# A recurrence kernel on one core: thirteen start loads folded to five, input and kernel pieces dealt out anew over the steps, and the products of zeros left out of the step loop

## What is computed

```python
# 1. a recurrence over time, h has 256 values for each sequence
xw = x @ Wx + b
for t in range(512): h = tanh(xw[:, t] + h @ Wh)
# 2. a long convolution; its kernel K is a sum of 64 decaying exponentials
K[m, t] = sum_n C_re[m, n] * exp(dt[m] * A[n] * t)
x = x + (h * K) + h * D
# 3. a gated scan (sigmoid gates, cumulative sums of logarithms)
# 4. 16 experts with top-2 routing, and one shared expert
```

## Time and profile before

| what | us |
|---|---|
| three timed runs | 998.55, 1029.65, 1040.39 (median 1029.65) |
| the profiled execution, device time | 1004.57 |
| its span from first to last instruction | 1002.7 |
| mean granted TensorE clock in it | 0.962 of full speed |

### The profile page before, as it was taken

One profiled execution on the slowest core, in us unless ns is written; L12 is line 12 of the kernel. 1 busy time (PEld: TensorE's weight loads), 2 busy tenths in 40 slices (PEclk: granted clock), 3 DMA queues, 4 the chain that ended last, 5 costly groups with the idle time before them and its releaser, 6 DMA issues.

```text
span 1002.7 us, 61045 instructions
## 1 busy us (share of the span) xinstructions
PE 938.8 (94%) x26800; PEld 768.1 (77%) x26800; DVE 437.5 (44%) x932; ACT 556.7 (56%) x1956; POOL 314.4 (31%) x308
## 2 busy tenths in 40 slices
PE   7999999999999997788999999999899999999994
PEld 5787777777777776577444444787899999999993
DVE  1000100010001006578398899975556464646450
ACT  3344454545544558687486767333466565656551
POOL 2111211121112112332000644573034546364555
PEclk6589999999999999899899999999999999999997
DMA  3122222234554402872100111163075757566534
GB/s 92 64 96 94 85 97 102 96 76 58 59 64 56 55 13 38 189 146 53 45 1 1 66 45 46 41 232 105 37 204 134 156 126 162 129 157 133 125 42 53
DMA packets 85347, 89.61 MB, mean 89 GB/s; under 512 B 8657, under 2 KB 71654, under 8 KB 85298
## 3 DMA queue, kind: packets, MB, share of 16 engines
q1 hardware_dynamic: 69410, 71.50, 28.3%
q0 software_dynamic: 14592, 17.10, 10.2%
q10 hardware_dynamic: 1296, 0.37, 0.2%
HBM read 56.82 MB, written 33.96 MB: 91 GB/s over the span
## 4 chain that ended last, share of the span: by engine, by line
PE 77%; issue 5%; ACT 5%; DVE 4%; POOL 4%; DMA 2%; ACTq 0%; POOLq 0%; DVEq 0%
PE ps L526 21%; PE ps L820 17%; PE ps L518 9%; PE ps L834 8%; PE ps L686 8%; PE ps L494 3%; PE ps L736 3%; POOL slots_in L457 3%; PE ps L501 2%; PE ps L745 2%; PE ps L593 2%; ACT tok L889 2%; PE ps L608 1%; DMA slots_in<-tok,arena 1%; PE ps L763 1%
## 5 line engine op out<-in xcount | busy, mean ns | idle before, releaser
L526 PE MATMUL ps<-tok,wh 128*32 128x8 f32 x16384 | 259.2, 182 | 13.5 <-issue 3.0
L526 PEld LDWEIGHTS ps<-tok,wh 128*32 128x32 f32 x16384 | 216.1, 115 | 61.2 <-ACT tok L889 25.6
L889 ACT ACTIVATE tok<-ps 128x8 f32<-128x8 f32 x1024 | 155.3, 177 | 190.1 <-PE ps L526 190.0
L476 POOL DMA_INDIRECT out<-arena,dest x80 | 127.9, 1599 | 99.3 <-ACT arena L1047 80.1
L1161 DVE TENSOR_SCALAR arena<-ps 128x127 f32<-128x127 f32 x32 | 9.3, 290 | 335.9 <-PE ps L501 335.9
L820 PE MATMUL ps<-xgT_hi,ew_hi 128*128 128x320 f32 (+1 forms) x384 | 119.5, 311 | 2.9 <-DVE spare L1302 1.6
L820 PE MATMUL ps<-xgT_hi,ew_lo 128*128 128x320 f32 (+1 forms) x384 | 119.8, 312 | 0.0
L820 PE MATMUL ps<-xgT_lo,ew_hi 128*128 128x320 f32 (+1 forms) x384 | 119.0, 310 | 0.0
L518 PE MATMUL ps<-xst,wx 128*32 128x64 f32 (+1 forms) x3120 | 106.7, 212 | 0.0
L1408 DVE TENSOR_TENSOR mid<-mid,ps 128x320 f32<-128x320 f32 (+1 forms) x96 | 46.7, 486 | 106.5 <-ACT mid L1065 104.4
L686 PE MATMUL ps<-mid,gw 128*128 128x512 f32 x192 | 86.1, 607 | 2.4 <-ACT mid L975 1.6
(11 more groups left out here) (206 smaller groups left out, 1760.7 us busy)
## 6 DMA issues: line engine op xcount, KB each, us to landing
ring<-k_pad SPq DMA_DIRECT2D x64, 256.0 KB, 6.3
slots_in<-mid SPq DMA_DIRECT2D x16, 645.0 KB, 3.6
mid<-slots_in SPq DMA_DIRECT2D x16, 645.0 KB, 4.2
arena<-in_ex_down SPq DMA_DIRECT2D x16, 384.0 KB, 3.2
arena<-in_ex_gate SPq DMA_DIRECT2D x16, 352.0 KB, 4.5
arena<-in_ex_up SPq DMA_DIRECT2D x16, 352.0 KB, 6.0
xst<-in_x_steps SPq DMA_DIRECT2D x66, 64.0 KB, 1.8
xtok<-in_x_tok SPq DMA_DIRECT2D x16, 256.0 KB, 2.7
```

The costliest lines, as they stand in the source:

```text
L476: pool.indirect_dma_start(out=out[:, :], out_offset=bass.IndirectOffsetOnAxis(ap=dest[:, z, t:t + 1], axis=0), in_=yo[:, z, t], in_offset= ...
L526: last = nc.tensor.matmul(sums_at(bank, t, o)[Q * j:Q * j + Q], wh[:, k, columns(j, o)], hring[:, (n - 1) % (2 * G), k], start=False, stop ...
L889: nc.scalar.activation(hring[:, n, o], sums_at(n // G, n % G, o), ACT.Tanh).then_inc(s_h[o], 1)
```

## The change

- Ten tables that came in ten loads (the first state `h0r` and the nine constants) lie side by side in one array `pack`, in DRAM and on chip, and come in one load of 128 rows by 737 floats, which ScalarE issues first. `wh` is loaded behind it, from ScalarE's queue and no longer from SyncE's, and `s_state` counts this load alone.
- VectorE copies the first state as soon as `pack` is there and clears `ctmp` after it.
- `keep_up(256)` is gone from the steps.
- The pieces of the inputs stand after other steps: 0 after t = 1, 1 and 2 after t = 2, 3 after t = 3, 4 and 5 after t = 4, 6 after t = 5, 7 and 8 after t = 6.
- The kernel sums stand after the steps 7 and 8, two pieces (four matmuls) each.

```diff
-        state = ((wh, wh_d), (h0r, h0_rec))
-        loads = ((a_q, a_q_d), (dt_q, dt_q_d), (a_bc, a_bc_d),
-                 (dt_bc, dt_bc_d), (c_q, c_q_d), (d_k, d_k_d), (consts, consts_d), (iota_t, iota_t_d), (rows_to, rows_to_d))
...
-        INPUTS = {1: (0, 2), 2: (2, 4), 3: (4, 5), 4: (5, 6), 5: (6, 7), 6: (7, NIN)}
+        INPUTS = {1: (0, 1), 2: (1, 3), 3: (3, 4), 4: (4, 6), 5: (6, 7), 6: (7, NIN)}
...
-            for dst, src in state:
-                sp.dma_start(dst[:], src).then_inc(s_state, 16)
...
-                    if t in (0, G - 1):
-                        keep_up(256)
-                    if 11 <= n < 11 + 2 * NH:
-                        if n == 11:
+                    if n in (G - 1, G):
+                        if n == G - 1:
                             pe.wait_ge(s_ps0, 1)
                             pe.wait_ge(s_kqe, i + 1)
                             pe.wait_ge(s_kc, i + 1)
-                        kernel_sums(n - 11)
-            pe.wait_ge(s_state, STATE_LOADED)
+                        for piece in range(NH * (n - G + 1), NH * (n - G + 2)):
+                            kernel_sums(piece)
+            pe.wait_ge(s_state, 16)
...
-            for dst, src in loads:
-                act.dma_start(dst[:], src).then_inc(s_const, 16)
+            act.dma_start(pack[:], pack_d).then_inc(s_const, 16)
+            act.dma_start(wh[:], wh_d).then_inc(s_state, 16)
...
-            nc.vector.memset(ctmp, 0.0).then_inc(s_x1, 2)
-
-            dve.wait_ge(s_state, STATE_LOADED)
+
+            dve.wait_ge(s_const, LOADED)
             for k in range(C):
                 nc.vector.tensor_copy(hring[:, 2 * G - 1, k], h0r[:, k]).then_inc(s_h[k], 1)
-            dve.wait_ge(s_const, LOADED)
+            nc.vector.memset(ctmp, 0.0).then_inc(s_x1, 2)
```

More of the change, by code:

```diff
@@ L51, with build @@
 AHEAD = EARLY - 1
-def build(nc, x_tok, x_steps, h0_rec, h0_gate, wx_d, wh_d, b_rec_d, a_bc_d, a_q_d, dt_bc_d, dt_q_d, c_q_d, d_k_d,
+def build(nc, x_tok, x_steps, h0_gate, wx_d, wh_d, b_rec_d, pack_d,
           gate_w, gate_b, router_w, router_b, sh_gate, sh_up, sh_down, ex_gate, ex_up, ex_down,
-          ident_d, consts_d, iota_t_d, tri_d, resets_d, iota_e_d, rows_to_d, out):
+          ident_d, tri_d, resets_d, iota_e_d, out):
     k_pad = nc.dram_tensor("k_pad", [D, 2 * P], F32).ap()
@@ L69, in build @@
         brow = sb("brow", [1, D])
-        h0r = sb("h0r", [P, C, B])
         h0g = sb("h0g", [P, C, B])
[L72 to L77, removed]
+        sizes = (C * B, NST, NH, NG * J, NG + KG, NG * NH, IT, 8, P, R + CT)
+        pack = sb("pack", [P, sum(sizes)])
+        h0r, a_bc, a_q, dt_bc, dt_q, c_q, d_k, consts, iota_t, rows_to = [pack[:, sum(sizes[:n]):sum(sizes[:n + 1])] for n in range(len(sizes))]
+        h0r = h0r.rearrange("p (c b) -> p c b", c=C)
+        dt_bc = dt_bc.rearrange("p (g j) -> p g j", j=J)
+        c_q = c_q.rearrange("p (g h) -> p g h", h=NH)
         dta_q = sb("dta_q", [P, NG + KG, NH])
@@ L83, in build @@
         ident = sb("ident", [P, P])
-        consts = sb("consts", [P, 8])
-        iota_t = sb("iota_t", [P, P])
         tri = sb("tri", [P, 2, P])
@@ L91, in build @@
         spare = sb("spare", [P, 512])
-        rows_to = sb("rows_to", [P, R + CT])
         share = sb("share", [P, 2, CT])
@@ L254, in build @@
         first = ((wx, wx_d), (brow, b_rec_d))
-        state = ((wh, wh_d), (h0r, h0_rec))
-        loads = ((a_q, a_q_d), (dt_q, dt_q_d), (a_bc, a_bc_d),
-                 (dt_bc, dt_bc_d), (c_q, c_q_d), (d_k, d_k_d), (consts, consts_d), (iota_t, iota_t_d), (rows_to, rows_to_d))
         late = ((ident, ident_d), (tri, tri_d), (h0g, h0_gate), (gw, gate_w), (gb, gate_b), (rw, router_w), (rb, router_b),
                 (resets, resets_d), (iota_e, iota_e_d))
-        FIRST_LOADED, STATE_LOADED, LOADED, LATE = 16 * len(first), 16 * len(state), 16 * len(loads), 16 * len(late)
+        FIRST_LOADED, LOADED, LATE = 16 * len(first), 16, 16 * len(late)
         NT = 2 * C
@@ L1484 @@
     tri = np.stack([np.triu(np.ones((P, P)), 1) - 1, np.ones((P, P))], 1).astype(f32)
+    pack = (rec(cond.T), np.broadcast_to(a_log, (P, NST)), np.tile(a_log.reshape(NH, Q).T, (J, 1)), np.broadcast_to(dt.reshape(J, NG).T, (P, NG, J)),
+            np.concatenate([np.repeat(dt.reshape(J, NG), Q, 0), np.zeros((P, KG), f32)], 1), c_re.reshape(J, NG, NH, Q).transpose(0, 3, 1, 2), d_k,
+            consts, np.broadcast_to(-np.arange(P, dtype=f32), (P, P)),
+            np.concatenate([np.arange(N, dtype=f32).reshape(P, R), N + np.arange(CAP, dtype=f32).reshape(P, CT)], 1))
     arrays = {
@@ L1487 @@
         "x_steps": np.concatenate([steps, np.zeros((2, P, C, G, B), f32)]),
-        "h0_rec": rec(cond.T),
         "h0_gate": rows(cond.T),
@@ L1492 @@
         "b_rec": np.asarray(L0_cond_b)[None],
-        "a_bc": np.broadcast_to(a_log, (P, NST)),
-        "a_q": np.tile(a_log.reshape(NH, Q).T, (J, 1)),
-        "dt_bc": np.broadcast_to(dt.reshape(J, NG).T, (P, NG, J)),
-        "dt_q": np.concatenate([np.repeat(dt.reshape(J, NG), Q, 0), np.zeros((P, KG), f32)], 1),
-        "c_q": c_re.reshape(J, NG, NH, Q).transpose(0, 3, 1, 2).reshape(P, NG, NH),
-        "d_k": d_k.reshape(P, IT),
+        "pack": np.concatenate([np.reshape(v, (P, -1)) for v in pack], 1),
         "gate_w": np.stack([rows(np.asarray(w).T) for w in (L0_cond2_W_f, L0_cond2_W_i, L0_cond2_W_h)], 1),
@@ L1509 @@
         "ident": np.eye(P, dtype=f32),
-        "consts": consts,
-        "iota_t": np.broadcast_to(-np.arange(P, dtype=f32), (P, P)),
         "tri": tri,
@@ L1514 @@
         "iota_e": np.broadcast_to(iota_e, (P, NE)),
-        "rows_to": np.concatenate([np.arange(N, dtype=f32).reshape(P, R), N + np.arange(CAP, dtype=f32).reshape(P, CT)], 1),
     }
```

## The result

The changed kernel takes 1043.59 us (median of four executions, 1040.21 to 1046.58) against 1021.56 for the kernel before (median of four, 998.55 to 1040.39). The ratio is 1.037 with a 95% interval from 1.023 to 1.051: it is slower. Unlike before, the four executions lie close together. The title's count of loads is off: before the loop 15 loads were issued, now 6, since ten became one.

A forecast was written before the change was run, and what follows sets the result against it. A two-engine ring of product and tanh, floor 0.67 us a step, bounds the loop. 1004.57 - 2.0 (start) - 9.0 (full-clock turns) - 2.4 (half-clock turns) = 991.2, plus 4 x 2.95 gives 1003 us; range 979 to 1077.

The forecast's parts named there:

- whether the clock comes back: TensorE's clock in the step loop: the rise to full clock was expected about as late as before; called the open term.
- the forecast of 1003: Whole kernel with six half-clock turns behind the first, the mean of before: 991.2 + 4 x 2.95 = 1003 us; chance 0.57.
- go for nothing at full clock: Products of zeros in the step loop: they stand where the distance is 0.67 us already, so removing them gains nothing.
- Rival A: Step loop: full clock does not come back, 29 more turns at half clock, 1077 us, slower by 4.6%; chance 0.18.
- account of its spread: Kernel before: its three timed runs fit about 0.3, 9 and 12 half-clock turns behind the first, 3.58 us a turn.
- Turns at half clock: Step loop: a turn becomes 13.8 us, 0.94 less (0.36 to 1.6); three such turns gain 2.4 us.
- Turns at full clock: Step loop: moved pieces and sums save 0.31 us a turn, to 10.85; 29 turns gain 9.0 us (0 to 12.8).
- The start: Before the loop: packed load brings the first tanh from 8.79 to 6.8 us, gain 2.0 us (0.7 to 2.1).
- chain of constants: ScalarE's start: pack lands at 5.0 us, the constants end at 6.5, so the products at 6.77 decide the first tanh.
- The first turn: Loop's first turn, partly stalled: counted among three half-clock turns gaining 2.4 us together; its stalls on issue stay.

The follow-up runs named there:

- the added branch: Twelve 512-column products of zeros behind a branch at the first turn's end: with zeros after steps 15 and 0 1024.58 us, kernel before 1030.93, changed kernel 1063.47.

## Why the prediction was wrong

**The step that failed** is the one on whether the clock comes back. I asked only when it rises, took it for granted that it then stays, and priced every case by one number of half-clock turns at the loop's start. I wrote down that the prediction fails altogether if the clock, once full, falls again inside the loop, and it fell six times: 20.3 half-clock turns behind the first, where the forecast of 1003 had six. What I had against the change ("the two steps around a turn's end have no fill any more") was the right place; I weighed it for the rise, where it is not what decides, and not for the hold. Runs with zeros back there and nowhere else kept the clock in all three profiles without the added branch. Where a rise would come I had right, behind the steps 7 to 10 of some turn.

**The clue in the rows.** The sum says that products of zeros "go for nothing at full clock", read from a distance of 0.67 that did not move. That is right for a turn and wrong for the kernel: the run without them shows the same 11.16 us turn and 66 us more in all. A matmul that nobody waits for had a use that no wait shows.

**Rival A** (no full clock in the loop) named the mechanism's family and was 33 us too high; the truth is between it and the forecast, with 20 half-clock turns behind the first instead of 31. No execution took more than the 1050 us that I had set for slower, but the 1029.65 behind that bound was too high for the kernel before; the ratio's interval, 1.023 to 1.051, says slower. The measured time lies inside the range of 979 to 1077, but the sign was wrong: I gave faster 0.45 and slower 0.22.

**The kernel before** itself had a median of 1021.56 with the fourth execution, and of 1005 to 1020 beside the later runs, not 1029.65. My account of its spread by when the rise comes fits the two profiles taken of this loop without the branch: rises at 56.0 and 115.4 us, four turns apart, which is 14 us at 3.58 a turn, and times 16 us apart.

**Turns at half clock**: 13.38 us, 0.94 was predicted as the gain and 1.36 measured, inside my 0.36 to 1.6. The zeros made 0.35 of it (14.39 us without them in the old places, 0.36 predicted), the new places the other 1.01, for which I had 0.6. **Turns at full clock**: 10.91, predicted 10.85. The floor holds behind steps 1, 2, 7 to 10, 13 and 14, better than the 0.70 that I took for 2 and 10; the back edge at 0.83 took 0.16 of it back, and I had no term for it.

**The start**: 2.0 us predicted, 0.44 measured in this pair of profiles, outside its 0.7 to 2.1. It varies: with the new start unaltered nine profiles have the first tanh at 7.51 to 8.58 us, mean 8.14, and three with the old one at 8.79 to 9.19, mean 8.98, so the gain is nearer 0.8. The pack landed early enough (ScalarE's first exponential at 4.17, I had 5.0), but I asked only whether `wh` would be late. What was late was the first input piece, which waits for `wx` among others: it came 0.87 us later and ran at half clock. The mechanism of the chain of constants was right; what was next to be late was not.

**The first turn** grew by 1.5 us where I had a small gain; its stalls on issue are longer or more (the one at 14.97 us took 0.79 before, the one at 15.79 now 1.43). It goes with the new start and not with the loop: in the run with the old loop and the new start the first turn takes 20.18 us, against 18.84 before and 20.30 in the changed kernel, and its second turn begins at 28.54 us where before it began at 27.63. So the earlier first tanh was more than lost again within the first turn. What makes the stalls longer no run tells.

The Trainium skill, "TensorE: Matmul & The Clock Gate", has in its section "A second HAM failure mode: psum-queue depth-cycling" a kernel whose short idles between groups of matmuls make the clock go to and fro, at a cost in throughput. The trace agrees: six falls between 81 and 368 us, with TensorE shown busy 16.15 of the 17.00 us before the first of them. The rule of its section "What's actually happening", that activity releases the clock, agrees with the twelve dense products, behind which it rose three times of three.

**What stays open.** Why the back edge costs 0.83 us in the changed loop and 0.67 in the loop of before; it is 0.67 in the run with ten zeros, so it is not the places of the pieces. Whether two products of zeros in other steps than 15 and 0 would hold the clock as well: no run puts them there, and what speaks for the place is where the falls come, the run that moved work to step 15, and the branch. What decides in which turn the rise comes (from 56 to 146 us in loops that then kept it), and why in single executions it seems not to have come at all. And whether the late rise can be had early without a branch: a second copy of the loop's code was not tried.

## What to carry to other kernels

Before a filler is taken out as useless, look at what the clock does in the kernel and not only at who waits for it: a loop whose engines wait for each other can be at the edge where TensorE's full clock is just held. Judge the thinnest stretch of a loop and its densest one apart; here falls came behind the first and rises behind the second. Put a filler into the empty steps first: two matmuls a turn held the clock as four did, for 0.17 us at half clock and nothing at full clock, and beside an input piece the same matmul cost 0.11 to 0.17 us each.

## What the runs showed of the hardware

- At full clock, TensorE shown as busy 95% of 17 us by the profile still fell to half clock; two matmuls of 0.28 us in a turn of 10.91 us kept it up for 243 us. A busy share of 95% in the profile is no sign that the full clock will stay.
- Behind the first turn 28 of 30 falls of the clock came 0.5 to 2.7 us behind the tanh of step 0, the thinnest place of the loop, and all 37 rises at the loop's fullest steps or just behind them.
- The full clock lasted 17 us each of the six times it fell in the changed loop, 37 us twice in the loop with one thin fill more, and mostly 3.4 us in the loop of before without zeros.
- Eight matmuls of 64 columns with 128-row weights cost no more than the floor of 0.67 us; four of them behind a piece of one-row weights cost 0.78.
- A branch on TensorE that is not taken cost 0.25 to 0.4 us in each turn.
- Twelve bf16 matmuls of 128 by 512 brought the full clock while they ran or right behind them, three times out of three.
